# Value products of two attention slots made together in every second slot

## The reference, cut to what matters

```python
q = einsum('oc,bct->bot', Wq, target) + bq     # 128 x 256
k = einsum('oc,bcs->bos', Wk, source) + bk
v = einsum('oc,bcs->bos', Wv, source) + bv
dot  = einsum('bhdt,bhds->bhts', q, k) / sqrt(8)
amap = softmax(mask * dot - (1 - mask) * 1e6) * mask
out  = einsum('bhts,bhds->bhdt', amap, v)      # the value products
```

## Time and profile before

| | us |
|---|---|
| median of three runs | 509.4 |
| the profiled execution | 509.36 |
| its span, first to last instruction | 507.6 |
| attention with both kinds of score, first reduce of batch 0's slots to last reduce | 180.3 to 341.2 |
| tail and start of the shared expert | 341.2 to 375 |
| TensorE clock granted, mean of the span | 0.997 of full |

### The profile page before, as it was taken

One profiled execution on the slowest core, in us unless ns is written; L12 is line 12 of the kernel. 1 busy time (PEld: TensorE's weight loads), 2 busy tenths in 40 slices (PEclk: granted clock), 3 DMA queues, 4 the chain that ended last, 5 costly groups with the idle time before them and its releaser, 6 DMA issues. The chain is left out here.

```text
span 507.6 us, 10286 instructions
## 1 busy us (share of the span) xinstructions
PE 474.1 (93%) x3384; PEld 259.3 (51%) x3384; DVE 381.3 (75%) x765; ACT 244.9 (48%) x461; POOL 230.1 (45%) x319
## 2 busy tenths in 40 slices
PE   2998999998999999999999998998999999999993
PEld 2663664854733633343343333333445647788882
DVE  4989889899888789999999999998465633333321
ACT  2761232332232078889999998787412010233331
POOL 3736434154755355867677763213010660042433
PEclk9999999999999999999999999999999999999998
DMA  7750175002775116566566655300022224378843
GB/s 237 216 176 0 43 166 89 2 0 62 186 195 150 54 57 174 147 171 184 162 163 172 171 153 147 84 5 5 1 94 77 74 94 166 120 185 195 192 112 41
DMA packets 67256, 59.96 MB, mean 118 GB/s; under 512 B 10048, under 2 KB 62256, under 8 KB 67216
## 3 DMA queue, kind: packets, MB, share of 16 engines
q1 hardware_dynamic: 63712, 55.24, 39.6%
q0 software_dynamic: 3072, 4.21, 4.9%
q10 hardware_dynamic: 432, 0.00, 0.0%
HBM read 38.90 MB, written 22.50 MB: 121 GB/s over the span
## 5 line engine op out<-in xcount | busy, mean ns | idle before, releaser
L1325 DVE TENSOR_REDUCE MX<-psum 128x2 f32<-128x512 f32 x256 | 162.1, 682 | 10.0 <-PE psum L1190 8.4
L1374 ACT ACTIVATE HP<-psum 128x512 f32<-128x512 f32 x224 | 122.1, 602 | 28.9 <-PE psum L1205 26.4
L1190 PE MATMUL psum<-QKA 60*128 60x256 bf16 x512 | 81.3, 273 | 7.1 <-DVE MX L1325 5.6
L1205 PE MATMUL psum<-QKA 60*128 60x256 bf16 x512 | 81.1, 273 | 1.5 <-DMA QKA<-max_scr 1.0
L1291 PE MATMUL psum<-HP,VP 128*32 128x256 f32 x1024 | 81.8, 391 | 0.3 <-issue 0.2
L602 PE MATMUL psum<-space_a,space_w 128*128 128x512 f32 x160 | 73.1, 602 | 1.9 <-DVE HP L629 1.9
L1190 PEld LDWEIGHTS psum<-QKA 60*128 60x128 bf16 x512 | 31.6, 94 | 63.8 <-DVE MX L1325 44.6
L1966 POOL DMA_INDIRECT out_x<-OE,to_u x16 | 24.9, 1557 | 62.6 <-ACT OE L2001 60.1
L602 PEld LDWEIGHTS psum<-space_a,space_w 128*128 128x128 f32 x160 | 29.0, 190 | 36.5 <-issue 31.0
L2089 PE MATMUL psum<-XT,WE 128*128 128x256 f32 (+1 forms) x192 | 44.0, 379 | 0.9 <-ACT XT L1985 0.9
L199 PE MATMUL psum<-space_a,wsh 128*128 128x512 f32 (+1 forms) x96 | 43.6, 598 | 0.3 <-PEq L1497 0.3
(11 more groups left out here) (207 smaller groups left out, 767.3 us busy)
## 6 DMA issues: line engine op xcount, KB each, us to landing
QKA<-stack_scr SPq DMA_DIRECT2D x32, 480.0 KB, 4.5
stack_scr<-PARTS SPq DMA_DIRECT2D x32, 192.0 KB, 2.1
WE<-in_W SPq DMA_DIRECT2D x16, 352.0 KB, 4.0
stack_scr<-PARTS SPq DMA_DIRECT2D x32, 128.0 KB, 2.0
XD<-dispatched SPq DMA_DIRECT2D x8, 258.0 KB, 3.9
X<-in_x SPq DMA_DIRECT2D x4, 512.0 KB, 5.8
CTX<-in_ctx SPq DMA_DIRECT2D x4, 512.0 KB, 8.2
MB<-in_mask SPq DMA_DIRECT2D x16, 128.0 KB, 3.3
```

The costliest lines, as they stand in the source:

```text
L1190: return pe.matmul(to[:, tt * T:(tt + 1) * T], QKA[rows, k, 0, h, tt * P:(tt + 1) * P], QKA[rows, k, 1, h, :], start=True, stop=True)
L1205: return pe.matmul(to[:, (m % 2) * T:(m % 2 + 1) * T], QKA[rows, k, 1, h, st * P:(st + 1) * P], QKA[rows, k, 0, h, :], start=True, stop=True)
L1325: dve.tensor_reduce(MX[:, par, head_of(n), :], src[:, :].rearrange("p (a s) -> p a s", a=2), axis=AX.X, op=ALU.max).then_inc(a_red, 1)
L1374: act.activation(PT[:, i % 2, st, 2 * half:2 * half + 2, :].rearrange("p j t -> p (j t)"), TBK3[THIRDS[m]], ACT.Exp).then_inc(a_exp, 1)
```

## The change

In slots with an odd p, `values` makes the calls of both slots of a pair, first st = 0, then st = 1; in slots with an even p it makes none. Slot 1 then makes the last two calls of the batch before, slot 3 those of slots 0 and 1, and so on to slot 7. Number, operands and order of the calls stay, and so does every wait.

```diff
                             def values():
-                                if i > 0 and there(b):
-                                    pe_pv(pe, g, k, i - 1, st)
-                                elif i == 0 and there(b, -1):
-                                    pe_pv(pe, *at(g, k, -1), 3, st)
+
+                                for of in range(2) if st == 1 else ():
+                                    if i > 0 and there(b):
+                                        pe_pv(pe, g, k, i - 1, of)
+                                    elif i == 0 and there(b, -1):
+                                        pe_pv(pe, *at(g, k, -1), 3, of)
```

## The result

The changed kernel took 515.71 us, median of five runs (515.60 to 516.62), against 509.40 before (509.26 to 510.41): +6.3 us, ratio 1.0123, 95% interval 1.0109 to 1.0137. Forecast were 518.2 and a range of 514.6 to 523.5. The profiled execution took 515.63 us with a span of 513.9 (before 509.36 and 507.6).

A forecast was written before the change was run, and what follows sets the result against it. TensorE and VectorE were taken to hold each other; -0.24 + 0.47 + 0.48 = +0.71 us a batch, 8.5 over twelve, + 0.5 + 0.2 - 0.7 + 0.3 = +8.8 on 509.4: 518.2 us, range 514.6 to 523.5.

The forecast's parts named there:

- The bound: Attention batches: TensorE and VectorE hold each other; VectorE sets the long middle of a batch, TensorE both ends.
- rival 1: Faster: TensorE is the bound and each merge saves two switches, about 499.8 us; chance 0.06.
- the tail: From batch 15's first tile TensorE is busy throughout; five merged visits save 0.7 us together.
- x: Pitch from one value-product call to a second directly following: taken as 0.48 us, range 0.44 to 0.64.
- A: Start of a batch, first to fourth plain score tile: 2.38 us becomes 2.14, change -0.24.
- B: From reduce 4 to reduce 8, two calls ahead of the reciprocal's transposes: 2.66 us becomes 3.13, change +0.47.
- D: From a batch's last plain score tile to the next batch's first, two calls between: 0.90 us grows by 0.48.
- C: From reduce 8 to the last score tile: VectorE gapless, later transposes and projection just covered, change 0.
- Rival 3: Slower by more: a second call does not close up, 0.57 us each, about +12.5, 521.9 us; chance 0.30.
- Batches at the edge: Batch 0 costs 0.5 us, batch 13 costs 0.2, batches 1 to 12 pay 0.71 each in full.

The follow-up runs named there:

- transposes first: Changed kernel with slot 3's four transposes issued ahead of its two value-product calls instead of behind them: 516.74 us, ratio to before 1.0144.
- the spread calls: Against the kernel before: batches 0 to 13 place value-product calls, none between a batch's last score tile and the next batch's first: 508.40 us.
- the spread calls with the end mended: The spread calls, but batch 13 keeps a call in slot 7 and batches 14 and 15 make pairs in odd slots: 505.79 us, ratio 0.9925.

## Why the prediction was right, and where it was off

*The bound.* Right. TensorE gave up busy time and the batch grew by 0.61 us; rival 1 (TensorE's own time counts, 499.8) is out, except in the tail. Every pair saves TensorE time: 1.00 us where two calls apart have 2 x 0.57 and two entries. It only buys time where no engine but TensorE is waited for. The Trainium skill (TensorEngine Tiling (Array Packing), Key Properties) states that changing the tiling mode drains TensorE. That this drain is what a pair saves isn't shown, and the prediction's "The rows agree with the rule in size" goes too far: no row has the drain by itself, and the transposed maxima follow a call after the same 0.57 (284.24 to 284.81) although their tile has the same 128*32 shape.

*The unknown x.* The term of the sum that was mis-sized. I took 0.48 and bounded it by 0.44 from below; the second call costs 0.43, and since x enters a batch three times, links A, B and D came out 0.05 to 0.06 lower each. A: S0 (288.08 in the trace after) to S3 (290.17) is 2.09, so -0.29, forecast -0.24. B: R4 to R8 is 3.08, +0.42 for +0.47. D: 1.32, +0.42 for +0.48. Sum with C's +0.02: +0.57 for +0.71, which is what this batch grew by, 11.54 to 12.11; over all batches it is +0.61. The timeline of single rounds shows what failed in the step. A round is four instructions, one for each group of columns; these are the second, third and fourth of the pair at 292.26:

```profile
292.50 0.40 PE L1291 MATMUL psum<-HP,VP 128*32 128x256 f32 x4
292.72 0.40 PE L1291 MATMUL psum<-HP,VP 128*32 128x256 f32 x4
292.93 0.40 PE L1291 MATMUL psum<-HP,VP 128*32 128x256 f32 x4
```

From the first round to the second it is 0.24, from then on 0.22 and 0.21. A single call has two rounds, so its rows show only the first pitch, and the prediction took that one for both rounds of the second call: 2 x 0.24 = 0.48 for a measured 0.43, which is two of the shorter ones. Rival 3, a second call that does not close up, is out by the same rows. The waits are smaller than forecast too: 0.28 us before the reciprocal for about 0.4, 0.54 to 0.61 before R0 for 0.7, and 12.17 a batch for 12.2 to 12.3.

*What the 2.5 us are made of.* The forecast was 2.5 us too high. Batches 2 to 12 grew by 6.7 us where 11 x 0.71 = 7.8 stood: 1.1, the size of x. Batch 1 makes 0.85 and the tail 0.5 (both below). So less than half of the miss is x. The upper end of the range is 523.1 by its own terms (521.9 and 12 x 0.1), not 523.5; nothing hangs on it.

*Link B's cause.* Half right: the size was, and I named both the late reciprocal and the missing tiles. The run with the transposes first shows that the tiles alone are enough and that turning the order gives nothing.

*Link C.* Right for this change: R8 to S15 is 4.59 us after, 4.57 before, and TensorE waits 0.40 us for the addition to x ahead of the projection without R14 being late. The run with slots 4 and 5 alone showed that the cover is thin: there R14 is late, S1 with it, and a batch costs 0.10.

*Batches at the edge.* The first reduce of batch 1's slots stood 10.22 us after batch 0's before, 10.77 after: +0.55 for 0.5. Batch 1 cost nothing (12.18 before, 12.04 after), where 0.71 stood in the sum. The prediction counted it as a full batch, but VectorE has more work in it: layer-norm statistics stand ahead of R6 (0.33 us, 194.78 to 195.11) and ahead of R14 (0.49 us, 201.10 to 201.59). Behind the wait before R0 the timeline after names no wait up to the next R0 at 203.00, not before the reciprocal either:

```profile
190.96 3.90 DVE L1325 TENSOR_REDUCE MX<-psum 128x2 f32<-128x512 f32 x6 [0.68 <-PE psum L1190]
```

So the late transposes and tiles find VectorE still at work. This is read from the trace; no run tests it. Batch 13 gave +0.21 for 0.2.

*The tail.* Right. VectorE's last reduce moved from 340.56 to 347.75 by 7.2 us, batch 15's first tile from 351.81 to 359.10 by 7.3, after an idle time that was still there (0.84 us on the load of the maxima, 1.01 before). From that tile to the end it took 154.8 instead of 155.8: -1.0 where the sum had -0.7 for the merges and +0.3 for ScalarE. No run shows that +0.3. From the last reduce to the end it is -0.9, so the tail as a whole was forecast 0.5 too high.

## What to carry to other kernels

Before moving work on one engine, mark in the timeline of one period where that engine waits for another one and where another waits for it. A visit moved into the stretch behind a bank wait costs its full length, one moved into a stretch where the next wait only gets shorter costs little or nothing, and one on an engine that is alone pays its saving: the same merge gave -0.14, +0.43, +0.10 and +0.32 us a batch in the four places. And a wait that the profile names is only the first thing late in its queue: before curing it, look how late the next one is.

## What the runs showed of the hardware that was not expected

Two value-product calls one behind the other need 1.00 us to the next work, a single one 0.57: the second adds 0.43, less than two rounds at the 0.24 that one call shows inside: from its second round on a pair has them 0.22 apart.

Gaps on TensorE can cost more than themselves. In four profiles its granted clock fell to 0.50 for a stretch in the attention: at 338.5 to 342 of the spread calls, after 0.74 us of work in two; in batch 0 of the spread calls with the end mended, after 1.40 in two, and in batch 0 of the run of slots 2 and 3 alone, after 1.35 in two; and in the run of slots 6 and 7 alone, at the turn from batch 12 to 13:

```profile
331.00:333.00 2.00, 1.34 (x16) 0.72 (x20) 1.80 (x4) 0.94 (x2) 0.00 (x0) 0.77 0.00 0
333.00:335.00 2.00, 2.00 (x23) 0.63 (x17) 0.47 (x1) 0.51 (x2) 0.00 (x0) 0.50 0.03 8
335.00:337.00 2.00, 2.00 (x25) 0.57 (x19) 1.50 (x3) 1.50 (x5) 0.59 (x2) 0.88 0.00 0
```

Its profiled run took 514.11 us, against 512.76 to 513.07 at the higher mean clock: 1.0 to 1.4 us, which go with one stretch. Only one execution of each kernel was traced; by the mean clocks of the others (0.995 or 0.996 in three, 0.991 and 0.989 in two) the same kernel has such a stretch in some executions and not in others. What lets the clock fall in one execution and not in another stays open. A change that frees TensorE but leaves the period to another engine can lose its gain in this way: the spread calls have the shortest period, 11.35 us (as they have with the end mended), and a median of 508.40.
